# Four layers on 28x28 images: where first-layer moments, kernel sums and channel scales stand in rows 0 to 4, and when row 0's second turn is made

## The chip, the core and the metric

The kernel runs on one core of a Trainium2 chip. The metric is the device time of one execution in microseconds (us). The core's engines work side by side and meet at semaphores: TensorE (PE in the profile, with its weight loads as PEld), VectorE (DVE), ScalarE (ACT), GpSimd (POOL) and the DMA queue of SyncE (SP). Each engine takes its own instructions strictly in the order of the program, so a wait holds everything behind it on that engine.

## The reference

Eight images of 28x28 tokens and 64 channels go through four residual layers, each behind a group norm:

```python
x = x + _L0_conv_ref(_gn(x), ...)   # shifted-window attention, 7x7 windows, 8 heads
x = x + _L1_conv_ref(_gn(x), ...)   # 3x3 convolution of signs, scaled by K * alpha
x = x + _L2_conv_ref(_gn(x), ...)   # 3x3 convolution with ternary weights
x = x + _L3_conv_ref(_gn(x), ...)   # gated projection with a 4-tap convolution
```

The change lies in the first layer, with three small pieces that it computes:

- the moments (mean, variance) of the group norm ahead of layer 0;
- `alpha = jnp.mean(jnp.abs(kernel), axis=(0, 1, 2))` of layer 1, the mean absolute value of its kernel for each output channel, which needs the kernel only and not x;
- the attention itself: `softmax(q k + bias + mask) v`, then a projection.

## The kernel before

The images lie as four pairs (`g` = 0 to 3), a pair's two images on partitions 0 to 63 and 64 to 127. A pair has four window rows of four windows, so the first layer is a loop over 16 rows, `R` = 0 to 15, and each row has two turns, `k = 2R` and `2R + 1`, which stand for the two halves of the heads and use two buffers of scores in PSUM (`k % 2`).

For a row, the steps run over the engines in this manner:

- POOL: `normalise(R)` writes the normed input `xn`; `mask_row(R)` spreads the keys over heads into `kex` (line 214, called from the loop as `mask_row(R + 2)`).
- PE: `proj_qk(R)` (L791) and `proj_v(R)` (L803) project; `scores(R)` (L820) adds q k to both score buffers of the row; `turn(k, j)` (L833) transposes half j of the scores of turn k into the PSUM bank `turned j`; `values(k)` (L853) multiplies the exponentials with v into the bank `outs`; `gather(R)` (L867) and `project(R)` (L876) finish the row.
- ACT: `seed(k)` (L510) writes the bias into the score buffer of turn k, and may do so only once DVE has read the buffer for turn k - 2 (`sub_done`); `scores(R)` waits for both of its row's seeds. `expo(k, j)` (L540) takes the exponential of what `turn(k, j)` wrote. `evac_qk` (L519, L520), `evac_v` (L530) and `evac_att` (L549) empty PSUM.
- DVE: `shift(k)` subtracts the maximum (reduction `mx`, L1196, then `d`, L1201); `weigh(R)` (L1210, L1215) divides by the sums; `residual(R)` (L1226) adds to x.

The three pieces that move are all issued by DVE between these steps. `window_moments(g)` (L1123 twice, then L1130) takes the moments of pair g from the window copy `xw`; those of pairs 2 and 3 come after `weigh(0)` in row 1, and `gn_stats` is raised after the second. `variances(2, 2, 3, mixed)` in row 2 turns what PE's `mix` made of them into two variances (L1157, L1160, L1162), for a power on POOL. `kernel_sums()` (L1247) reduces the absolute kernel, which ACT wrote into `h1` in row 1, to `asum`. It comes right behind the variances in row 2. PE then makes `alpha` from `asum` with one matmul (L912, in row 3 behind `scores(4)`), in spare columns of the bank `turned 1`, which is why it waits until the exponential of the last turn there has been read (`exp_done`). `channel_scales()` (L1256 twice) copies `alpha` into `aw`; it is DVE's first step in row 4, and `turn(7, 1)` on PE, which overwrites that bank, waits for it (`aw_ready`). `aw` is used only behind the 16 rows, in `channel_sums`.

PE's order in a row R above 0 is: `turn(2R, 0)`, `turn(2R, 1)`, `values(2R - 1)`, `proj_v(R + 1)`, `scores(R + 1)`, `turn(2R + 1, 0)`, `turn(2R + 1, 1)`, `gather(R - 1)`, `values(2R)`, `proj_qk(R + 3)`, `project(R - 1)`. ACT's order in a row is: both `expo(2R, j)`, `evac_v(R + 1)`, both `expo(2R + 1, j)`, `evac_att(R - 1)`, `evac_qk(R + 3)`, `seed(2R + 4)`, `seed(2R + 5)`. In row 0 ACT has `seed(3)` and `evac_qk(2)` in the place of the first `evac_v`.

The order is written out by hand; no planner decides it.

Of the kernel before, what the change touches and what calls it, by code (L numbers as in the profile page):

```python
# [50 lines left out]
def program(nc, x_in, xw_in, cst_in, wts_in, late_in, ker1_in, ker2_in, rel_in, out):  # L51
    ctx = ExitStack()
    with ctx:
# [18 lines left out]
        def cc(name):  # L72
            a, n = CI[name]
            return cst[:, a:a + n]
# [44 lines left out]
        asum = sb("asum", [P, C])  # L119
# [30 lines left out]
        def sems(names):  # L150
# [12 lines left out]
        bqs_ready, pe_bt, bt_ready, kabs_ready, asum_ready, pe_alpha = sems(  # L163
            "bqs_ready pe_bt bt_ready kabs_ready asum_ready pe_alpha")
# [35 lines left out]
        NR = NG * NW  # L200
# [548 lines left out]
        def _(pe):  # L749
# [29 lines left out]
            def proj_qk(R):  # L779

                pe.wait_ge(xn_ready, R + 1)
                if R > 0:
                    pe.wait_ge(q_ready, R)
                    pe.wait_ge(ks_ready, R)
                if R > 0:
                    pe.wait_ge(v_ready, max(R - 1, 1))
                if R >= 4:
                    pe.wait_ge(att_ready, R - 3)
                rhs = xn[:, R % 4]
                for n, name in enumerate(("wq", "wk")):  # L790
                    mm = pe.matmul(ps_qk[:, n * RT:(n + 1) * RT], ww(name), rhs, start=True, stop=True)  # L791
                mm.then_inc(qk_done, 1)

            def proj_v(R):

                pe.wait_ge(xn_ready, R + 1)
                pe.wait_ge(q_ready, 1 if R == 0 else min(R + 2, NR))
                pe.wait_ge(ks_ready, 1 if R == 0 else min(R + 2, NR))
                if R == NR - 1:
                    pe.wait_ge(att_ready, R - 2)  # L800
                for a in range(NW):
                    for e in range(2):
                        mm = pe.matmul(ps_qk[64 * e:64 * e + WT, a * C:(a + 1) * C], xn[:, R % 4, a],  # L803
                                       ww("wv")[:, e * C:(e + 1) * C], start=True, stop=True)
                mm.then_inc(v_done, 1)
# [19 lines left out]
            def turn(k, j):  # L825
                pe.wait_ge(sub_done, k + 1)
                if k > 0:
                    pe.wait_ge(exp_done, 2 * k - 1 + j)
                if k == 7 and j == 1:
                    pe.wait_ge(aw_ready, 1)  # L830
                for n in range(4):
                    h = 8 * j + 2 * n
                    mm = pe.transpose(ps_t[j][0:WK, n * WQ:n * WQ + WK],  # L833
                                      d[0:WK, k % 2, h:h + 2, :].rearrange("p a b -> p (a b)")[:, 0:WK], packed)
                mm.then_inc(t_done, 1)

            def values(k):
                R, p = k // 2, k % 2
                pe.wait_ge(exp_done, 2 * k + 2)
                if p == 0:  # L840
                    pe.wait_ge(v_ready, R + 1)
                    if R > 0:
                        pe.wait_ge(o_ready, R)
                    if R > 1:
                        pe.wait_ge(res_done, R - 1)
                    pe.wait_ge(gn_copied, copied_by(R))

                for a in range(2):
                    for j in range(2):
                        for hp in range(2):  # L850
                            n = 8 * a + 4 * p + 2 * j + hp
                            for c in range(2):
                                mm = pe.matmul(ps_o[64 * c:64 * c + WT, 18 * n:18 * n + 18],  # L853
                                               pt[0:WK, k % 2, j, 2 * a + hp, WT * c:WT * c + WT],
                                               vsb[0:WK, R % 2, 2 * (4 * (2 * a + c) + 2 * j + hp) + p, :],
                                               start=True, stop=True)
                mm.then_inc(pv_done, 1)

            def gather(R):

                pe.wait_ge(o_ready, R + 1)
                pe.wait_ge(v_ready, min(R + 3, NR))
                if R >= NR - 2:
                    pe.wait_ge(att_ready, R)

                for m in range(NW // 2):
                    mm = pe.transpose(ps_qk[:, m * WQ:m * WQ + WK],  # L867
                                      osb[0:WK, 2 * m:2 * m + 2].rearrange("p a c -> p (a c)"), packed)
                mm.then_inc(ot_done, 1)

            def project(R):
                pe.wait_ge(att_ready, R + 1)
                pe.wait_ge(o_ready, R + 1)
                if R > 0:
                    pe.wait_ge(res_done, R)
                pe.matmul(ps_x, ww("wp"), att[:].rearrange("p i m j -> p (i m j)"), start=True, stop=True)\  # L876
                  .then_inc(proj_done, 1)
# [14 lines left out]
            for R in range(NR):  # L892
                g, r = R // NW, R % NW

                turn(2 * R, 0)
                turn(2 * R, 1)
                if R == 0:
                    proj_qk(2)
                if R == 2:
                    mix(2, 2, 3, mixed)  # L900
                if g > 0 and r == 2:
                    mix(col(1, g - 1), 1, nth(1, g - 1), mixed)
                if R > 0:
                    values(2 * R - 1)
                if 0 < R < NR - 1:
                    proj_v(R + 1)
                if R + 1 < NR:
                    scores(R + 1)
                if R == 3:
                    pe.wait_ge(asum_ready, 1)  # L910
                    pe.wait_ge(exp_done, 14)
                    pe.matmul(alpha, cc("ones"), asum[:], start=True, stop=True).then_inc(pe_alpha, 1)  # L912
                turn(2 * R + 1, 0)
                turn(2 * R + 1, 1)
                if R == 0:
                    proj_v(1)
                else:
                    gather(R - 1)
                values(2 * R)
                if R + 3 < NR:  # L920
                    proj_qk(R + 3)
                if R > 0:
                    project(R - 1)

            def conv_bank(u):

# [188 lines left out]
        def _(dve):  # L1115
# [4 lines left out]
            def window_moments(g):  # L1120

                for i in range(2):
                    last = dve.bn_stats(st[:, g % 2, i, :], xwflat[:, g, i * HALF:(i + 1) * HALF])  # L1123
                last.then_inc(bn_done, 1)
                dve.wait_ge(bn_done, g + 1)
                return merge(g % 2, col(0, g))
# [123 lines left out]
            def channel_scales():  # L1250

                dve.wait_ge(init_pool, 2)
                dve.wait_ge(pe_alpha, 1)
                for w in range(2):
                    q = slice(64 * w, 64 * w + 64)
                    last = dve.tensor_scalar(aw[q, 64 * w:64 * w + 64], alpha[q],  # L1256
                                             4.0 / (NTAP * C) / (NTAP * C), None, ALU.mult)
                last.then_inc(aw_ready, 1)
# [6 lines left out]
            for R in range(NR):  # L1265
                g, r = R // NW, R % NW

                if R == 4:
                    channel_scales()
                shift(2 * R)  # L1270
                shift(2 * R + 1)
                if R >= 1:
                    weigh(R - 1)
                if R >= 2:
                    if R == 2:
                        dve.wait_ge(ld_xu, 16)
                    residual(R - 2)
                if R == NR - 1 or g > 0 and r == 0:
                    dve.wait_ge(res_done, R - 1)
                    first_moments(g - 1 + (R == NR - 1))  # L1280
                if R == 0:
                    variances(1, 1, 2, mixed)
                if R == 1:
                    dve.wait_ge(ld_x2, 16)
                    window_moments(2)
                    window_moments(3).then_inc(gn_stats, 1)
                if R == 2:
                    variances(2, 2, 3, mixed)
                    kernel_sums()
                if g > 0 and r == 1:  # L1290

                    dve.wait_ge(res_done, R - 1)
                    last_moments(g - 1).then_inc(gn_stats, 1)
                if g > 0 and r == 2:
                    variances(col(1, g - 1), 1, nth(1, g - 1), mixed)
                if g > 0 and r == 3:
                    if g == 1:
                        dve.wait_ge(init_pool, 3)
                    signs(g - 1)
# [220 lines left out]
```

## Time and profile before

| | before |
|---|---|
| median of 3 runs | 196.95 us (196.94 to 197.01) |
| profiled execution, its own time | 196.93 us |
| span of its instructions | 195.1 us |
| PE busy | 182.3 us (93%) |
| DVE busy | 155.4 us (80%) |
| ACT busy | 128.3 us (66%) |
| POOL busy | 107.7 us (55%) |
| granted TensorE clock | 1.0 of full speed in every slice |

The 16 rows of the first layer take the span from about 15 to 119 us. The time of the profiled execution is 1.8 us more than the span, and that part lies outside all instructions. The shares are means over stages with different limits, so the stretch of rows 0 to 4 (15 to 50 us) has to be read by itself. In the rows of the timeline the columns are: start (us), busy time (us), engine, line, operation, output and inputs, count, and in brackets the idle time before it on that engine with what ended it. Where DVE instructions follow each other, the start of one may lie up to a tenth before the end of the one ahead.

### The profile page before, as it was taken

Reading aid. Unit: us, or ns where it says so; the run is one execution under the profiler, and the core shown is the slowest. Engines: PE = TensorE matmul, PEld = TensorE weight load, DVE = VectorE, ACT = ScalarE, POOL = GpSimd, SP = SyncE. Lnnn points to the kernel's source line nnn. Section 1 sums busy time; section 2 is a strip of 40 time slices with the busy share of each in tenths; the row PEclk is TensorE's granted clock in tenths of the full one; section 3 lists DMA queues with packets and bytes.
Section 4 is the critical chain, followed back from the end, with each engine's and each line's share of the span. In section 5 each row is a group of like instructions: output and inputs, shape, how many; then the busy total and the mean of one; then the engine's idle time right before and its main releaser. Section 6 shows DMA issues by size and latency. Waiting matters only on the chain.

```text
span 195.1 us, 6785 instructions
## 1 busy us (share of the span) xinstructions
PE 182.3 (93%) x2751; PEld 130.8 (67%) x2751; DVE 155.4 (80%) x322; ACT 128.3 (66%) x251; POOL 107.7 (55%) x122
## 2 busy tenths in 40 slices
PE   7876989989999999999999999998899999999994
PEld 2445878878898889889987886664456655453330
DVE  3568798978899788987898893799997768957653
ACT  3346778569767997777977757154965339789650
POOL 0339999958432479644595107749644410647560
PEclk9999999999999999999999999999999999999999
DMA  6990000000000000000000000002234521011512
GB/s 190 430 403 12 3 0 5 5 3 2 3 3 3 3 3 3 2 3 3 5 3 3 0 3 3 0 3 47 49 85 112 132 57 41 0 45 30 176 57 107
DMA packets 5021, 9.97 MB, mean 51 GB/s; under 512 B 768, under 2 KB 3840, under 8 KB 4864
## 3 DMA queue, kind: packets, MB, share of 16 engines
q1 hardware_dynamic: 4848, 9.21, 15.1%
q8 instruction: 22, 0.36, 0.7%
q10 hardware_dynamic: 144, 0.34, 0.4%
q14 instruction: 7, 0.06, 0.1%
HBM read 5.03 MB, written 1.61 MB: 34 GB/s over the span
## 4 chain that ended last, share of the span: by engine, by line
PE 74%; DVE 15%; issue 3%; POOL 3%; DMA 2%; ACT 2%; DVEq 0%; ACTq 0%; POOLq 0%
PE turned L833 13%; PE outs L853 12%; PE scores L954 7%; PE scores L820 6%; PE qkv L791 5%; PE turned L1036 4%; PE scores L1010 3%; PE scores L970 3%; PE qkv L803 3%; PE qkv L1024 3%; DVE mx L1196 3%; PE scores L1011 3%; DVE d L1201 3%; PE outs L876 2%; DMA xw<-xw_in 2%
## 5 line engine op out<-in xcount | busy, mean ns | idle before, releaser
L833 PE MATMUL turned<-cst,d 113*113 113x113 f32 x256 | 32.6, 270 | 2.3 <-DVE d L1201 2.0
L214 POOL TENSOR_TENSOR kex<-ks,cst 128x784 f32<-128x784 f32 (+1 forms) x16 | 23.6, 1472 | 19.9 <-ACT ks L519 19.3
L833 PEld LDWEIGHTS turned<-cst,d 113*113 113x113 f32 x256 | 28.6, 178 | 7.8 <-issue 4.7
L510 ACT ACTIVATE scores<-rel 113x784 f32<-113x784 f32 x32 | 26.0, 827 | 10.9 <-DVE d L1201 6.0
L540 ACT ACTIVATE pt<-turned 113x392 f32<-113x392 f32 x64 | 28.3, 493 | 6.3 <-PE turned L833 6.3
L1201 DVE TENSOR_TENSOR d<-scores,mx 113x784 f32<-113x784 f32 x32 | 31.2, 976 | 1.1
L1196 DVE TENSOR_REDUCE mx<-scores 113x16 f32<-113x784 f32 x32 | 30.7, 959 | 1.8 <-PE scores L820 1.7
L853 PE MATMUL outs<-vsb,pt 113*49 113x18 f32 x1024 | 29.2, 199 | 0.2 <-ACT pt L540 0.2
L853 PEld LDWEIGHTS outs<-vsb,pt 113*49 113x49 f32 x1024 | 26.1, 125 | 4.2 <-issue 0.6
L340 POOL TENSOR_TENSOR rstd<-ve,mhalf 128x1 f32<-128x1 f32 (+1 forms) x15 | 8.7, 580 | 24.3 <-DVE ve L1162 24.0
L249 POOL TENSOR_TENSOR kex<-su,sz 128x392 f32<-128x392 f32 x14 | 14.0, 1018 | 12.2 <-ACT su L664 7.1
L519 ACT ACTIVATE ks<-qkv,wts 128x196 f32<-128x196 f32 x16 | 6.8, 422 | 15.7 <-PE qkv L791 15.7
L820 PE MATMUL scores<-kex,qs 32*49 32x196 f32 x512 | 14.6, 332 | 2.4 <-ACT scores L510 1.9
L791 PE MATMUL qkv<-xn,wts 128*128 128x196 f32 x64 | 14.7, 352 | 0.3 <-ACT vsb L530 0.3
L1210 DVE RECIPROCAL rc<-outs 113x32 f32<-113x32 f32 x16 | 5.7, 358 | 10.9 <-PE outs L853 10.8
L939 PE MATMUL scores<-sg,w 128*128 128x392 bf16 x72 | 13.2, 332 | 0.5 <-DVE sg L1262 0.5
L1349 DVE SCALAR_TENSOR_TENSOR su<-scores,late,su 128x392 f32<-128x392 f32 x24 | 13.2, 619 | 0.4
L530 ACT ACTIVATE vsb<-qkv 49x256 f32<-49x256 f32 x32 | 12.6, 395 | 1.1 <-PE qkv L803 0.9
L377 POOL TENSOR_TENSOR h<-ab 128x840 f32<-128x840 f32 x4 | 6.3, 1586 | 12.6 <-ACT ab L558 12.5
L954 PE MATMUL scores<-p,w 128*64 128x392 bf16 x144 | 13.2, 334 | 0.0
L820 PEld LDWEIGHTS scores<-kex,qs 32*49 32x49 f32 x512 | 9.1, 117 | 4.7 <-issue 4.0
L1226 DVE SCALAR_TENSOR_TENSOR x<-outs,bt,x 128x175 f32<-128x175 f32 (+5 forms) x40 | 9.6, 290 | 1.9 <-PE outs L876 1.9
(130 smaller groups left out, 376.1 us busy)
## 6 DMA issues: line engine op xcount, KB each, us to landing
p<-parts SPq DMA_DIRECT2D x14, 112.5 KB, 2.2
x<-x_in SPq DMA_DIRECT2D x1, 1568.0 KB, 9.9
out<-xw SPq DMA_DIRECT2D x8, 196.0 KB, 1.9
xs<-xs SPq DMA_DIRECT2D x8, 98.5 KB, 2.1
xw<-xw_in SPq DMA_DIRECT2D x2, 392.0 KB, 4.7
xw<-xw_in SPq DMA_DIRECT2D x1, 784.0 KB, 6.6
ker<-ker_in SPq DMA_DIRECT2D x2, 288.0 KB, 10.3
p3x<-parts SPq DMA_DIRECT2D x8, 60.0 KB, 2.0
```

The lines of the kernel that those rows point to most:

```text
L214: return engine.tensor_tensor(kex[:, par, :, a * WT:b * WT], ks[:, a * WT:b * WT].rearrange("p (o t) -> p o t", o=1).broadcast_to([P, 4, n ...
L249: engine.tensor_tensor(yy[:, u % 4, :], su[:, u % 8], sz[:, u % 8], ALU.mult)\
L510: act.activation(o, i, ACT.Identity).then_inc(seeded, 1)
L540: act.activation(pt[0:WK, k % 2, j].rearrange("p n (w t) -> p n w t", w=2), ps_t[j][0:WK, 0:4 * WQ].rearrange("p (n w t) -> p n w t", n=4, ...
L791: mm = pe.matmul(ps_qk[:, n * RT:(n + 1) * RT], ww(name), rhs, start=True, stop=True)
L820: mm = pe.matmul(ps_s[w][64 * c:64 * c + WT, j, a * 4 * WT:(a + 1) * 4 * WT], qs[q, R % 2, m:m + WT], kex[q, R % 2, :, m:m + WT], start=Fa ...
L833: mm = pe.transpose(ps_t[j][0:WK, n * WQ:n * WQ + WK], d[0:WK, k % 2, h:h + 2, :].rearrange("p a b -> p (a b)")[:, 0:WK], packed)
L853: mm = pe.matmul(ps_o[64 * c:64 * c + WT, 18 * n:18 * n + 18], pt[0:WK, k % 2, j, 2 * a + hp, WT * c:WT * c + WT], vsb[0:WK, R % 2, 2 * (4 ...
L939: mm = pe.matmul(ps[:, 0:HALF], w1[:, tap, :], sg1[:, g, ky + i * HR:ky + (i + 1) * HR, kx:kx + HW], start=(tap == 0), stop=(tap == NTAP - 1))
L954: pe.matmul(ps[64 * w:64 * w + 64, 0:HALF], w2[:, tap], p12[:, g % 2, w, ky + i * HR:ky + (i + 1) * HR, kx:kx + HW], start=(tap == 0), sto ...
L1196: dve.tensor_reduce(top, sc, AXX, ALU.max).then_inc(max_done, 1)
L1201: dve.tensor_tensor(d[0:WK, s].rearrange("p (j m) t -> p j m t", j=2)[:, :, :, 0:WT], sc, top.rearrange("p j (m o) -> p j m o", o=1).broad ...
```

## The change

Five things move, and nothing is added or left out.

1. DVE takes `window_moments(2)` (with its wait for the load of pairs 2 and 3) in row 0 behind the variances of pair 1; `window_moments(3)` stays in row 1.
2. `kernel_sums()` goes from row 2 to the end of row 3.
3. `channel_scales()` goes from the front of row 4 to its end, behind `weigh(3)`, `residual(2)` and `first_moments(0)`. `turn(9, 1)` instead of `turn(7, 1)` waits for it.
4. PE's matmul for `alpha` goes from row 3, behind `scores(4)`, to row 4, ahead of `scores(5)`. It waits for `exp_done` 18, which is `expo(8, 1)`, where it waited for 14, `expo(6, 1)`.
5. In row 0 PE makes `turn(1, 0)` and `turn(1, 1)` ahead of `scores(1)`, not behind it.

```diff
@@ turn
-                if k == 7 and j == 1:
+                if k == 9 and j == 1:
                     pe.wait_ge(aw_ready, 1)
@@ the loop over rows, PE
                 if R == 0:
                     proj_qk(2)
+                    turn(1, 0)
+                    turn(1, 1)
+                    scores(1)
+                    proj_v(1)
+                    values(0)
+                    proj_qk(3)
+                    continue
...
-                if R > 0:
-                    values(2 * R - 1)
-                if 0 < R < NR - 1:
+                values(2 * R - 1)
+                if R < NR - 1:
                     proj_v(R + 1)
+                if R == 4:
+                    pe.wait_ge(asum_ready, 1)
+                    pe.wait_ge(exp_done, 4 * R + 2)
+                    pe.matmul(alpha, cc("ones"), asum[:], start=True, stop=True).then_inc(pe_alpha, 1)
                 if R + 1 < NR:
                     scores(R + 1)
-                if R == 3:
-                    pe.wait_ge(asum_ready, 1)
-                    pe.wait_ge(exp_done, 14)
-                    pe.matmul(alpha, cc("ones"), asum[:], start=True, stop=True).then_inc(pe_alpha, 1)
                 turn(2 * R + 1, 0)
                 turn(2 * R + 1, 1)
-                if R == 0:
-                    proj_v(1)
-                else:
-                    gather(R - 1)
+                gather(R - 1)
                 values(2 * R)
...
@@ the loop over rows, DVE
-                if R == 4:
-                    channel_scales()
                 shift(2 * R)
                 shift(2 * R + 1)
...
                 if R == 0:
                     variances(1, 1, 2, mixed)
-                if R == 1:
                     dve.wait_ge(ld_x2, 16)
                     window_moments(2)
+                if R == 1:
                     window_moments(3).then_inc(gn_stats, 1)
                 if R == 2:
                     variances(2, 2, 3, mixed)
+                if R == 3:
                     kernel_sums()
+                if R == 4:
+                    channel_scales()
```

## Rows read from the trace of the kernel before

**Rows 1.** Windows: stretch, its length, busy us of each engine (instructions), PEclk, DMA.
```profile
15.00:21.40 6.40, 4.91 (x100) 4.13 (x100) 5.43 (x9) 4.80 (x10) 6.04 (x9) 1.00 0.01 3
...
28.00:35.00 7.00, 6.52 (x136) 5.45 (x136) 6.41 (x14) 5.42 (x12) 6.72 (x5) 1.00 0.02 5
...
66.00:72.00 6.00, 6.00 (x137) 5.31 (x129) 5.32 (x10) 5.55 (x13) 2.68 (x2) 1.00 0.01 3
```
**Rows 2.** Timeline of row 0, ACT, DVE and PE.
```profile
17.05 0.83 ACT L510 ACTIVATE scores<-rel 113x784 f32<-113x784 f32 x1 [0.26 <-DVE d L1201]
...
17.19 0.98 DVE L1162 SCALAR_TENSOR_TENSOR ve<-sg 128x1 f32<-128x1 f32 x1
...
18.03 0.91 PE L820 MATMUL scores<-kex,qs 32*49 32x196 f32 x32 [1.12 <-ACT scores L510]
```
**Rows 3.** Timeline of row 1, PE and DVE.
```profile
21.93 0.98 DVE L1201 TENSOR_TENSOR d<-scores,mx 113x784 f32<-113x784 f32 x1
...
24.79 0.91 PE L820 MATMUL scores<-kex,qs 32*49 32x196 f32 x32 [0.27 <-ACT scores L510]
...
24.82 1.02 DVE L1123 BATCH_NORM_STATS2 st<-xw 128x6 f32<-128x392 f32 x2
...
27.15 0.92 DVE L1196 TENSOR_REDUCE mx<-scores 113x16 f32<-113x784 f32 x1
```
**Rows 4.** Timeline of row 2, PE, DVE and POOL.
```profile
29.13 1.05 PE L833 MATMUL turned<-cst,d 113*113 113x113 f32 x8 [0.23 <-DVE d L1201]
...
31.85 1.49 POOL L214 TENSOR_TENSOR kex<-ks,cst 128x784 f32<-128x784 f32 x1
...
32.80 0.57 DVE L1160 TENSOR_SCALAR negm<-sg 128x2 f32<-128x2 f32 x1
```
**Rows 5.** Chain that ended last, end of row 2: start us, us, what.
```profile
33.65 1.09 DVE asum L1247
```
**Rows 6.** Timeline of row 3 and of the front of row 4, PE, DVE and POOL.
```profile
38.67 0.73 POOL L340 TENSOR_TENSOR rstd<-ve,mhalf 128x2 f32<-128x2 f32 x1
...
39.35 0.54 DVE L1226 SCALAR_TENSOR_TENSOR x<-outs,bt,x 128x175 f32<-128x175 f32 x2
...
39.53 0.91 PE L820 MATMUL scores<-kex,qs 32*49 32x196 f32 x32 [0.48 <-ACT scores L510]
...
39.74 1.49 POOL L214 TENSOR_TENSOR kex<-ks,cst 128x784 f32<-128x784 f32 x1
...
40.37 0.43 PE L912 MATMUL turned<-asum,cst 128*128 128x64 f32 x2
...
40.64 0.60 PE L833 MATMUL turned<-cst,d 113*113 113x113 f32 x4
40.92 0.46 DVE L1256 TENSOR_SCALAR aw<-turned 64x64 f32<-64x64 f32 x2 [1.02 <-PE turned L912]
...
41.41 0.97 DVE L1196 TENSOR_REDUCE mx<-scores 113x16 f32<-113x784 f32 x1
...
41.52 0.62 PE L833 MATMUL turned<-cst,d 113*113 113x113 f32 x4 [0.28 <-DVE aw L1256]
```
**Rows 7.** Timeline of row 4 and of the front of row 5, PE, ACT and DVE.
```profile
44.21 0.96 PE L833 MATMUL turned<-cst,d 113*113 113x113 f32 x8
...
46.05 0.36 DVE L1210 RECIPROCAL rc<-outs 113x32 f32<-113x32 f32 x1 [0.78 <-PE outs L853]
...
46.20 0.88 ACT L540 ACTIVATE pt<-turned 113x392 f32<-113x392 f32 x2
...
46.42 0.91 PE L820 MATMUL scores<-kex,qs 32*49 32x196 f32 x32
...
47.27 1.05 PE L833 MATMUL turned<-cst,d 113*113 113x113 f32 x8
...
47.85 0.96 DVE L1196 TENSOR_REDUCE mx<-scores 113x16 f32<-113x784 f32 x1
...
50.38 0.95 PE L833 MATMUL turned<-cst,d 113*113 113x113 f32 x8
```

More of the change, by code:

```diff
@@ L921, in _ @@
                     proj_qk(R + 3)
-                if R > 0:
-                    project(R - 1)
+                project(R - 1)
             def conv_bank(u):
```

## The prediction

> **What bounds the kernel now.** I read the windows first. From 66 to 72 us PE is busy for 6.00 of 6.00 us: late in the 16 rows TensorE sets the pace, and an event that comes earlier there stays earlier to the end. From 28 to 35 us PE has idle time (6.52 of 7.00), while DVE holds 6.41 and POOL 6.72 [rows 1]. So time can be won in rows 0 to 4 alone, and only what is left of a gain when the PE-bound rows begin, at `turn(9)` and `turn(10)`, counts. The tempo to compare with is that of row 4: `turn(8)` 44.21, `scores(5)` 46.42, `turn(9)` 47.27, `turn(10)` 50.38 [rows 7], that is 2.21 + 0.85 + 3.11 = 6.17 us a row.
>
> The chain and the timeline then say what stands in the way in rows 0 to 4. In row 0 PE waits 1.12 us for `seed(3)` ahead of `scores(1)` [rows 2]. In row 1 DVE holds two window moments from 24.82 until `mx(4)` at 27.15, with `scores(2)` (24.79 + 0.91) long done [rows 3]; `turn(4)` on PE then waits for DVE [rows 4]. In row 2 `kernel_sums` alone takes 1.09 us of the chain [rows 5]. In row 3 PE loses 40.37 to 40.64 to the alpha matmul, and `turn(7, 1)` waits for `aw` until 41.52 [rows 6].
>
> **Row 0: the turn ahead of the scores.** `seed(3)` and `turn(1)` are released by the same `d(1)`; the seed runs from 17.05 to 17.88 and `scores(1)` starts at 18.03 [rows 2]. Put first, `turn(1)` fills PE from about 17.1 to 18.0, under the wait that is there anyway. So `scores(1)` stays at 18.0 to 18.05, and what stood behind it on PE (`proj_v(1)`, `values(0)`, `proj_qk(3)`, `turn(2)`) comes some 0.9 us earlier as far as its inputs allow. Its queue on ACT gains with it: `expo(1)` no longer waits for a late turn. Cost: nothing, with `seed(3)` as the cover; without that cover it would be 0.9 us of delay for `scores(1)`.
>
> **Row 0: the moments of pair 2.** Two window moments fill 24.82 to 27.15, so one costs 1.17 [rows 3]. Its wait for the load of pairs 2 and 3 costs nothing: from 15 us on the DMA engines are busy for 0.01 of the time [rows 1], so the load is in. Behind the variances, whose last instruction ends at 17.19 + 0.98 = 18.17, it ends at about 19.3. `scores(1)` is done at 18.03 + 0.91 = 18.94 [rows 2], so `mx(2)` comes 0.25 us later than now. That is all that it costs, and it goes down the DVE chain: `d(3)` ends at 22.91 + 0.25 = 23.15 [rows 3], `seed(5)` is 0.83 long as in [rows 2] and ends at 24.0, and `scores(2)` starts 0.15 later, at 24.15 instead of 24.79.
>
> **Row 1.** `mx(4)` now waits for `scores(2)` alone: 24.15 + 0.91 + 0.1 = 25.15, two us earlier than 27.15. With that `turn(4)` no longer waits for DVE; PE's own order sets it: 24.15 + 0.85 + 3.11 = 28.1 against 29.13 [rows 4, 7]. What is late next is PE, and the gain is 1.0.
>
> **Row 2: POOL's spread of the keys.** From `turn(4)` by way of `values(3)`, `weigh(1)` and `residual(0)` to `negm` of the variances are 3.67 us [rows 4]; moved, `negm` would start at 28.1 + 3.67 = 31.8. But now `negm` took 0.57 us for two columns, and it ended at 33.37, just behind POOL's `kex`, which ran from 31.85 to 33.34 [rows 4]. I read this as DVE being held until POOL was done, and POOL's instruction doesn't move: POOL is full there [rows 1] and nothing of its queue changes. The Trainium skill ("SBUF — State Buffer", its passage on reading the diagram of the two sides) says that DVE and GpSimd share a port pair as an exclusive lock, which a DVE instruction in a two-port mode or with two SBUF inputs needs; the 0.57 us bears this out, and by that rule the three variance instructions behind `sg` are held again. Without such a lock they would be over at about 32.4, and the time would be that of the first rival.
>
> So I take it that the variances end at about 33.65, as they do now [rows 5], whatever rows 0 to 2 have won before. What remains of the gain is that `kernel_sums` isn't there: `shift(6)` starts 1.09 us earlier. This is the main term. It also says that the reorder in row 0 and the moved moments win little by themselves: they buy room that ends at POOL. If `negm` slips in ahead of `kex` and only what follows it is held, another 0.1 is won.
>
> **Row 3.** `scores(4)` waits for `seed(9)`, that for `d(7)` [rows 6]; all of it moves by 1.09, to 38.44. `residual(1)` ends at 39.35 + 0.54 - 1.09 = 38.80 [rows 6], `kernel_sums` follows and ends at 39.89. `scores(4)` ends at 39.35, so `mx(8)` starts at 39.85 instead of 41.41, late by 0.4 against what it could be. The bounds of `kernel_sums` here are 0.7 (576 columns at the rate of `mx`, 0.97 us for 784 [rows 6]) and 1.17 us (as it ran, with the overlap of its neighbours); I take 1.09, the row itself. PE has lost its alpha matmul (0.27) and the wait of `turn(7, 1)`: half a turn from 40.64 ends at about 41.06, and it was held until 41.52, so 0.46. `turn(7)` is at 38.44 + 0.85 = 39.29 and `turn(8)` at 39.29 + 3.11 = 42.40, 1.8 us earlier than 44.21. What is late next is DVE and ACT.
>
> **Row 4: alpha in front of the scores.** This part takes most of it back. `mx(8)` at 39.85 and four instructions of 0.97 and 0.98 (with their overlap 3.88) give `d(9)` at 43.73; `seed(11)` ends at 44.60. Without alpha, `scores(5)` could start at 44.75. Now alpha stands in front and waits for `expo(8, 1)`, which ACT has only behind `seed(11)`: the pair of exponentials takes 0.88 [rows 7], so it ends at 45.4; with 0.1 for the semaphore alpha starts at 45.5, and 0.27 later [rows 6] `scores(5)` at 45.8. Queued behind on PE are `scores(5)` and both halves of `turn(9)`; on DVE `mx(10)` waits for it, at 46.8 (now 47.85 [rows 7]). The price is 1.05, bounded by 0.9 (the exponentials alone) and 1.2 (alpha at its full 0.43 [rows 6]). `turn(9)` starts at 45.8 + 0.85 = 46.65 against 47.27: the gain is 0.6 to 0.65.
>
> `turn(9, 1)`, half a turn later at 47.05, now waits for `aw`. `rc` of `weigh(3)` follows `turn(8)` by 1.84 and the end of `first_moments(0)` follows `rc` by 1.80 [rows 7]: 42.40 + 3.64 = 46.04. Alpha is there at 45.5 + 0.43 + 0.1 = 46.03, and `channel_scales` takes 0.46 [rows 6], though POOL's `kex` ran beside part of it: `aw` is ready for PE at 46.6, 0.4 us early. On DVE nothing is queued behind it but `shift(10)`, which waits for `scores(5)` anyway.
>
> **The sum.** Rows 0 to 2 bring 1.09 to `shift(6)`; in row 3 that grows to 1.56 at `mx(8)`, 1.8 at `turn(8)`; alpha gives back 1.05 to 1.15; at `turn(9)` 0.65 is left. From there on PE is busy throughout [rows 1], and all queues move together. The profiled execution took 196.93 us (span 195.1 and 1.8 around it; the median is 196.95): 196.93 - 0.65 = 196.3 us.
>
> **Rivals.**
>
> *The variances pass POOL.* If DVE reached `negm` some 0.5 us earlier than 31.8, or if the 0.57 us is no lock, variances end at about 32.4. Then row 3 is no longer tied to 33.65: `turn(6)` is PE's, at about 34.7, `mx(8)` at 38.9, and `turn(9)` 0.95 earlier than forecast. That gives 195.3. Against it is [rows 4], for it only that 31.8 and 31.85 are near each other.
>
> *`turn(9, 1)` waits for `aw`.* The wait of row 3 moves into row 4. It decides from 0.4 us of lateness on DVE. At the size of today (0.46 [rows 6]) the gain shrinks to 0.2: 196.7, no change. For it: four DVE steps stand in front, and alpha comes late; against it: the 0.4 us.
>
> *`kernel_sums` is held by POOL.* In row 3 it comes at 38.80, and POOL starts `rstd` at 38.67 and `kex` at 39.74 to 41.23 [rows 6]. Were the reduction, which reads SBUF, held like `negm` until that run is over, it would start 2.45 us late, and `mx(8)`, the seeds, alpha and `turn(9)` would follow one for one: 196.3 + 2.45 = 198.7, slower. It decides from whether a reduction with one SBUF input needs what POOL holds, and from its coming behind 38.67. Against it: 1.09 us beside a POOL that is busy for 6.72 of 7.00 us [rows 1, 5]. The Trainium skill ("VectorE: DVE Perf Modes", the perf-mode tier table) has a reduction in the one-port mode only, which speaks against it too.
>
> **How the numbers follow.** Forecast 0.64, variances pass 0.10, `aw` wait 0.18, `kernel_sums` held 0.08. The forecast's own range is 196.0 (0.1 from `negm`, 0.15 from alpha at its lower bound) to 196.6 (alpha at 1.2 and `mx(2)` felt later on). The range goes from 195.8 to 196.9, which takes in the forecast and the `aw` wait and leaves out most of the other two. A measurement of this kernel can tell 0.2% (0.4 us) from no change. Faster by more: 0.70, from the forecast without its upper edge (0.60) and the first rival; within: 0.22, from the `aw` wait and that edge; slower: 0.08.
>
> **What would show it.** `scores(1)` at 18.0 behind `turn(1)`; `mx(2)` at 19.3; `turn(4)` near 28.1; `negm` or `ve` ending at POOL's 33.34; `mx(6)` at 33.6; a PE wait of about 0.9 us ahead of L912 at 45.5, ended by ACT's exponential; no wait at `turn(9, 1)`; `turn(9)` near 46.6. It is wrong if `mx(6)` starts before 33, if alpha doesn't wait, or if rows 5 to 15 lose the gain again.

## The result and the profile after

The changed kernel took 195.57 us (four executions, 195.43 to 195.60) against 196.94 for the kernel before: a ratio of 0.9929, with an interval of 0.9911 to 0.9946. That is 1.37 us faster. 196.3 had been forecast, in a range of 195.8 to 196.9, and the time of the first rival was 195.3: the direction was right, the range missed the time by 0.23 us on the fast side, and the case that came was the one given a chance of 0.10. The profiled execution took 195.60 us with a span of 193.8.

A later set of twelve executions of the same kernel (changed_again, below) gave 196.06 against 196.97, a ratio of 0.9951 (0.9943 to 0.9960). The 196.06 lies inside the forecast's range, and only one of the times, 195.45, is like those of the first set. What sorts these times is the main question of this text. The sets of runs were taken on several chips, on which the kernel before took 196.94 to 197.06, so differences of about 0.1 us between sets say nothing. In the sets below, executions in which the granted clock fell under 0.995 (one here, three of ten in port_free, two of ten in sums_in_row2) are left out of the groups that are named, since they are 1 to 2.5 us longer.

The windows of the kernel after, with the same columns as [rows 1]:

```profile
28.00:35.00 7.00, 7.00 (x145) 6.43 (x144) 5.58 (x13) 5.68 (x13) 6.72 (x5) 1.00 0.02 5
35.00:41.50 6.50, 6.50 (x141) 5.75 (x140) 5.80 (x10) 4.53 (x11) 6.18 (x6) 1.00 0.02 5
41.50:48.00 6.50, 5.04 (x130) 4.26 (x129) 5.34 (x11) 4.79 (x11) 4.59 (x9) 1.00 0.02 4
```

PE is now busy from 28 to 41.5 us without a gap (6.52 of 7.00 in the first stretch before), and then idles for 1.5 us: that is row 4.

The timeline of rows 0 and 1 after, answering to [rows 2, 3, 4]. `seed(3)` starts at 17.27 here and at 17.05 before, so 0.22 us of each time below is only a later start of everything:

```profile
17.29 1.05 PE L833 MATMUL turned<-cst,d 113*113 113x113 f32 x8 [0.16 <-DVE d L1203]
...
18.27 0.91 PE L820 MATMUL scores<-kex,qs 32*49 32x196 f32 x32
...
19.50 0.92 DVE L1198 TENSOR_REDUCE mx<-scores 113x16 f32<-113x784 f32 x1
...
24.33 0.91 PE L820 MATMUL scores<-kex,qs 32*49 32x196 f32 x32 [0.47 <-ACT scores L510]
...
25.34 0.96 DVE L1198 TENSOR_REDUCE mx<-scores 113x16 f32<-113x784 f32 x1
...
28.28 0.96 PE L833 MATMUL turned<-cst,d 113*113 113x113 f32 x8
```

The turn stands in front of `scores(1)`, which starts at once behind it; `mx(4)` is 2.0 us earlier than before, `turn(4)` 1.1, both counted from `seed(3)`.

Row 2 after, answering to [rows 4]:

```profile
31.86 0.20 DVE L1162 TENSOR_SCALAR negm<-sg 128x2 f32<-128x2 f32 x1
31.93 0.34 DVE L1164 SCALAR_TENSOR_TENSOR ve<-sg 128x1 f32<-128x1 f32 x2
32.11 1.53 POOL L214 TENSOR_TENSOR kex<-ks,cst 128x784 f32<-128x784 f32 x1
32.19 0.97 DVE L1198 TENSOR_REDUCE mx<-scores 113x16 f32<-113x784 f32 x1
...
34.81 0.96 PE L833 MATMUL turned<-cst,d 113*113 113x113 f32 x8
```

Here the forecast parts from what happened. `negm` takes 0.20 instead of 0.57, both `ve` are over at 32.27, and it is POOL's spread of the keys that is a little longer (1.53 against 1.49). `mx(6)` starts at 32.19 and not at 33.82, which is the forecast's 33.6 with the later start. The prediction had named `mx(6)` before 33 as a sign that it was wrong.

Rows 3 and 4 after, answering to [rows 6, 7]:

```profile
37.85 1.16 DVE L1249 TENSOR_REDUCE asum<-h 128x64 f32<-128x576 f32 x1
...
38.92 0.96 DVE L1198 TENSOR_REDUCE mx<-scores 113x16 f32<-113x784 f32 x1
...
40.04 1.50 POOL L214 TENSOR_TENSOR kex<-ks,cst 128x784 f32<-128x784 f32 x1
...
41.63 0.42 ACT L519 ACTIVATE ks<-qkv,wts 128x196 f32<-128x196 f32 x1 [1.91 <-POOL kex L214]
...
42.26 1.57 ACT L510 ACTIVATE scores<-rel 113x784 f32<-113x784 f32 x2
...
43.75 0.88 ACT L540 ACTIVATE pt<-turned 113x392 f32<-113x392 f32 x2
...
44.77 0.41 PE L916 MATMUL turned<-asum,cst 128*128 128x64 f32 x2 [1.46 <-ACT pt L540]
...
45.11 0.91 PE L820 MATMUL scores<-kex,qs 32*49 32x196 f32 x32
45.29 0.46 DVE L1258 TENSOR_SCALAR aw<-turned 64x64 f32<-64x64 f32 x2 [0.53 <-PE turned L916]
...
45.96 1.05 PE L833 MATMUL turned<-cst,d 113*113 113x113 f32 x8
```

Alpha waits 1.46 us for the exponential, with `scores(5)` queued behind it, while the seeds were done at 43.83. `turn(9)` goes through in one piece, since `aw` is ready at 45.75. It comes 1.53 us earlier than before (45.96 against 47.27, and the 0.22 of the start).

### The profile page after: what moved, and what is told of

It reads as the page before. It is cut to its first block, busy times and chain, and to the rows that moved or that the text cites. A ratio compares the mean times of both kernels' runs of the same rounds, so it can differ in the third digit from the quotient of the medians.

```text
span 193.8 us, 6785 instructions
## 1 busy us (share of the span) xinstructions
PE 182.7 (94%) x2751; PEld 131.0 (68%) x2751; DVE 154.9 (80%) x322; ACT 128.0 (66%) x251; POOL 107.8 (56%) x122
## 4 chain that ended last, share of the span: by engine, by line
PE 80%; DVE 12%; POOL 3%; issue 2%; ACT 2%; ACTq 0%; DVEq 0%; POOLq 0%
PE turned L833 14%; PE outs L853 13%; PE scores L820 7%; PE scores L956 7%; PE qkv L791 6%; PE turned L1038 4%; PE scores L1012 3%; PE scores L972 3%; PE qkv L803 3%; PE qkv L1026 3%; PE outs L876 3%; PE scores L765 3%; PE scores L1013 3%; DVE mx L1198 2%; DVE d L1203 2%
## 5 line engine op out<-in xcount | busy, mean ns | idle before, releaser
L803 PE MATMUL qkv<-wts,xn 128*49 128x64 f32 x256 | 10.2, 221 | 1.0 <-ACT qs L520 1.0
```

## Experiments

Two theories stood against each other. One: POOL holds DVE's variances if it comes first, and the whole surplus over the forecast is that in this kernel DVE came first by a tenth of a us. The other: nothing is held, and the gain is simply PE's and DVE's earlier work.

**late_variances** puts DVE half a us later at the point of meeting.

```diff
                 if R == 2:
+                    dve.bn_stats(st[:, 1, 1, :], xwflat[:, 2, 0:HALF])
                     variances(2, 2, 3, mixed)
```

> The changed kernel with one more statistics instruction of 0.51 us on DVE ahead of the variances of pairs 2 and 3 in row 2; its result goes to a buffer that nobody reads any more. In the changed kernel the three variance instructions run from 31.86 to 32.27 and POOL's spread of the keys starts at 32.11. Theory (DVE only passed POOL by a tenth, and is held by it if it comes second): negm starts near 32.4, one of the variance instructions ends at POOL's end (33.65), mx(6) starts near 33.9 instead of 32.19, turn(6) near 36.0 instead of 34.81, turn(9) near 46.9 instead of 45.96, and the time is 196.4 to 196.6. Rival (nothing holds DVE; the 0.57 us of before was something else): mx(6) starts 0.5 later at 32.7, d(6) ends at 34.7, just in time for turn(6) at 34.81, and the time stays at 195.6 to 195.7.

Measured: 196.37 us (196.27 to 196.58), ratio 0.9967 (0.9955 to 0.9978). Its timeline in row 2:

```profile
31.52 0.56 DVE L1288 BATCH_NORM_STATS2 st<-xw 128x6 f32<-128x392 f32 x1
...
31.93 1.49 POOL L214 TENSOR_TENSOR kex<-ks,cst 128x784 f32<-128x784 f32 x1
32.00 0.15 DVE L1159 TENSOR_TENSOR sg<-outs,epsv 128x6 f32<-128x6 f32 x1
32.18 1.27 DVE L1162 TENSOR_SCALAR negm<-sg 128x2 f32<-128x2 f32 x1
...
33.36 0.37 DVE L1164 SCALAR_TENSOR_TENSOR ve<-sg 128x1 f32<-128x1 f32 x2
...
33.65 0.96 DVE L1198 TENSOR_REDUCE mx<-scores 113x16 f32<-113x784 f32 x1
...
35.68 1.05 PE L833 MATMUL turned<-cst,d 113*113 113x113 f32 x8 [0.86 <-DVE d L1203]
```

`negm`, 0.17 to 0.20 us long when free, takes 1.27 and ends at 33.45, behind POOL's 33.42. Counted from `seed(3)` (17.12 here), half a us of delay became 1.6 at `mx(6)`; `turn(6)` then waits 0.86 us for DVE, and 0.8 is left in the time, against the first set of the changed kernel. `sg`, which reads PSUM, ran beside the same POOL instruction in 0.15 us without being held; the statistics did too, but had started ahead of it. The rival (195.6 to 195.7) is out.

**row0_as_before** undoes the reorder alone: `scores(1)` again ahead of `turn(1)`.

```diff
                     proj_qk(2)
-                    turn(1, 0)
-                    turn(1, 1)
                     scores(1)
+                    turn(1, 0)
+                    turn(1, 1)
                     proj_v(1)
```

> The changed kernel with row 0 in the old order: scores(1) ahead of turn(1). Theory (the reorder is what brings DVE past POOL): turn(4) comes near 29.0 instead of 28.28, negm near 32.5, behind the start of POOL's spread at 32.1, is held until 33.65, and the time is 196.3 to 196.6, so that the reorder by itself is worth 0.8 to 1.0 us. Rival, as in the prediction (the reorder only buys room that is lost later): 195.6. Third case (the reorder is worth its PE time, without any holding): turn(6) 0.6 later and 196.0 to 196.2.

Measured: 196.40 us (196.26 to 196.49), ratio 0.9966 (0.9954 to 0.9978). `negm` starts at 32.43, POOL at 31.99, and `negm` is held for 1.07 us. Against the first set of the changed kernel the reorder is worth 0.8, and 0.3 against the later one (196.06), where a part of the variances is held as well. So the prediction's "win little by themselves" is wrong for it where DVE passes. The trace shows the hold; what the old order would cost without one was not run.

**moments_in_row1** undoes the move of `window_moments(2)` alone.

```diff
                 if R == 0:
                     variances(1, 1, 2, mixed)
+                if R == 1:
                     dve.wait_ge(ld_x2, 16)
                     window_moments(2)
-                if R == 1:
                     window_moments(3).then_inc(gn_stats, 1)
```

> The changed kernel with window_moments(2) back in row 1, beside that of pair 3; row 0 keeps its new order. mx(4) then waits for DVE until about 26.5 instead of 25.34 and turn(4) comes 0.2 to 0.3 later, which puts negm at about 32.1, level with POOL's spread. Theory (this part is worth what it does for that meeting): DVE comes second in most executions and the time is 196.2 to 196.5, with 195.6 to 195.8 where it comes first. Rival (the part is worth nothing, PE covers it): 195.4 to 195.6.

Measured: 196.28 us (196.10 to 196.40), ratio 0.9963 (0.9951 to 0.9976). `negm` starts at 31.90 and POOL at 31.93; `negm` takes 0.17 us and the two `ve` take 1.59. Against changed_again, of the same set of runs, that is 0.22 us, with a hold in both. The 0.7 against the first set is therefore mostly the difference between the changed kernel's own two times, and it isn't shown that this move decides between them.

**sums_in_row2** undoes the move of `kernel_sums`, the prediction's main term.

```diff
                 if R == 2:
                     variances(2, 2, 3, mixed)
-                if R == 3:
                     kernel_sums()
```

> The changed kernel with kernel_sums back in row 2, right behind the variances; alpha and the channel scales stay in row 4. The prediction called this move the main term, 1.09 us: by that the time would be 196.6. Theory now: in row 2 it delays mx(6) by 1.09, but turn(6) only by 0.5, since PE is the later one there; in row 3 it is gone and mx(8) waits for scores(4) instead of it; seeds, alpha and turn(9) come 0.3 to 0.4 later than in the changed kernel, and the time is 195.9 to 196.0.

Measured: a median of 197.18 us, ratio 0.9996 (0.9968 to 1.0024), but in two groups: three executions at 195.74 to 195.92 and five at 197.0 to 197.27. The profiled one is of the second group (197.2):

```profile
31.75 0.17 DVE L1162 TENSOR_SCALAR negm<-sg 128x2 f32<-128x2 f32 x1
31.82 1.66 DVE L1164 SCALAR_TENSOR_TENSOR ve<-sg 128x1 f32<-128x1 f32 x2
31.97 1.49 POOL L214 TENSOR_TENSOR kex<-ks,cst 128x784 f32<-128x784 f32 x1
...
33.40 1.14 DVE L1249 TENSOR_REDUCE asum<-h 128x64 f32<-128x576 f32 x1
```

`negm` got through, and the second of the two `ve` was held until POOL's 33.46 (they end at 33.48). The same program is faster or slower by 1.3 us, with POOL starting 0.22 us behind `negm` here and 0.25 in the kernel after. The lower group fits the 195.9 expected for a free DVE; that it was free there is inferred from the time, since no trace of that group was taken.

**changed_again** is the changed kernel without an edit.

> The changed kernel, unaltered, in more executions. In four executions DVE's variances passed POOL's spread of the keys by a tenth of a us and the time was 195.4 to 195.6; in sums_in_row2 the same meeting went both ways in one kernel (195.8 or 197.1). Theory (a meeting so near goes both ways by chance): most executions at 195.4 to 195.6, and those that lose it near 196.4, as late_variances. Rival (in this kernel DVE always wins): all at 195.4 to 195.6.

Measured: 196.06 us, ratio 0.9951 (0.9943 to 0.9960). One execution took 195.45, nine 195.90 to 196.15, one 196.37. The profiled one took 195.92:

```profile
31.57 0.17 DVE L1162 TENSOR_SCALAR negm<-sg 128x2 f32<-128x2 f32 x1
31.65 1.63 DVE L1164 SCALAR_TENSOR_TENSOR ve<-sg 128x1 f32<-128x1 f32 x2
31.78 1.49 POOL L214 TENSOR_TENSOR kex<-ks,cst 128x784 f32<-128x784 f32 x1
33.21 0.96 DVE L1198 TENSOR_REDUCE mx<-scores 113x16 f32<-113x784 f32 x1
...
35.23 1.05 PE L833 MATMUL turned<-cst,d 113*113 113x113 f32 x8 [0.55 <-DVE d L1203]
```

POOL follows `negm` by 0.21 us, and a `ve` is held. The meeting does go both ways, as the first theory has it, but the expectation failed: most executions took neither of its two times. The middle case (`negm` passes and only what is behind it is held) stands in the prediction, at 0.1 us, and I left it out of the expectation. Counted from `seed(3)`, `mx(6)` starts 0.3 us earlier here than in late_variances. By these times the change brings 1.4 us where all three pass, and 0.9 where a `ve` is held; only two of the fifteen executions have a trace. All four of the first set took 195.43 to 195.60, and one of eleven of the second did, so it is not an even chance from one execution to the next; what differed between the sets is not known.

**port_free** takes away what holds DVE: POOL's sign weights leave rows 1 and 2, and its spread of the keys runs three us earlier.

```diff
...
-                if R == 1:
-                    binary_signs()
-                if R == 2:
+                if R == 3:
                     ternary_signs()
                 if R == 4:
+                    ternary_rest()
                     tap_weights()
+                if R == 5:
+                    binary_signs(0)
+                if R == 9:
+                    pool.wait_ge(xn_ready, R + 5)
+                    binary_signs(1)
```

> The changed kernel with POOL's sign weights moved out of rows 1 and 2 (the binary halves to rows 5 and 9, the ternary steps to rows 3 and 4). POOL's spread of the keys for row 4 then runs near 28.6 to 30.1, long before DVE's variances at 31.9, so that nothing is left there to meet. Theory: every execution has the variances free; ACT's emptying of the keys of row 6 no longer waits for POOL (it did for 1.91 us of idle time, of which 0.7 beyond PE), but scores and alpha in row 4 are then bound by d(9), so only 0.1 to 0.2 is won: 195.35 to 195.55. Rival (POOL's full queue is a bound of its own in rows 2 to 4): below 195.2.

Measured: a median of 195.46 us, ratio 0.9941 (0.9915 to 0.9967); the seven executions at a clock of 0.998 or more took 195.19 to 195.53, one group. So ACT's wait for POOL ahead of row 6's keys, 1.91 us of idle time in the profile after, is worth no more than 0.2.

**late_variances_port_free** is that and late_variances together.

> As port_free, with the additional 0.51 us statistics instruction of late_variances ahead of the variances. Theory (late_variances lost 0.8 us because POOL held DVE, not because DVE was later): with POOL's spread gone from that place the delay costs nothing, since PE is the later one at turn(6): 195.35 to 195.7. Rival (the half us of DVE itself is what cost): 196.2 to 196.4, as late_variances.

Measured: 195.47 us (195.33 to 195.65), ratio 0.9917 (0.9902 to 0.9932). Its row 2:

```profile
32.45 0.17 DVE L1169 TENSOR_SCALAR negm<-sg 128x2 f32<-128x2 f32 x1
32.53 0.34 DVE L1171 SCALAR_TENSOR_TENSOR ve<-sg 128x1 f32<-128x1 f32 x2
32.79 0.97 DVE L1205 TENSOR_REDUCE mx<-scores 113x16 f32<-113x784 f32 x1
...
34.93 0.95 PE L840 MATMUL turned<-cst,d 113*113 113x113 f32 x8
```

The same half us of DVE costs 0.8 with POOL's `kex` in the way and nothing without (195.47 against 195.46). So what made it dear is POOL's instruction in that place, and not DVE's lateness.

**alpha_behind_scores** prices the other disputed term by putting alpha behind `scores(5)`.

```diff
-                if R == 4:
-                    pe.wait_ge(asum_ready, 1)
-                    ...
                 if R + 1 < NR:
                     scores(R + 1)
+                if R == 4:
+                    pe.wait_ge(asum_ready, 1)
+                    ...
```

> The changed kernel with alpha behind scores(5) instead of ahead of it; turn(9, 1) still waits for the channel scales. Theory (alpha ahead of the scores costs PE a wait of over one us for the exponential): scores(5) starts near 44.0 instead of 45.11, alpha near 44.8, turn(9) near 45.1, its second half waits for the channel scales until about 45.9 where it started at 46.4, and the time is 195.0 to 195.2. Rival (the wait only stands where another one would: the scores or the channel scales are late anyway): 195.5 to 195.7.

Measured: 195.12, 195.15, 195.65 and 195.76 us, ratio 0.9918 (0.9901 to 0.9935). The two upper times fit a held `ve`, which was not traced. In the profiled execution (195.12) the variances pass POOL, and row 4 goes:

```profile
43.90 0.91 PE L820 MATMUL scores<-kex,qs 32*49 32x196 f32 x32 [0.64 <-ACT scores L510]
...
44.74 0.43 PE L918 MATMUL turned<-asum,cst 128*128 128x64 f32 x2
45.01 0.60 PE L833 MATMUL turned<-cst,d 113*113 113x113 f32 x4
...
45.89 0.62 PE L833 MATMUL turned<-cst,d 113*113 113x113 f32 x4 [0.28 <-DVE aw L1258]
```

`scores(5)` is 1.2 us earlier; a turn that waits for `aw`, as in [rows 6], takes more than half of that back: the lower two times are 0.45 us under the changed kernel's first set.

**alpha_at_the_end** moves alpha into row 15, behind `turn(30)`, into a bank of scores that is free by then, and `channel_scales` behind `shift(31)`.

```diff
-        alpha = ps_t[1][:, 4 * WQ:4 * WQ + C]
+        alpha = bk[0][:, 0:C]
...
+                if R == NR - 1:
+                    pe.wait_ge(asum_ready, 1)
+                    pe.matmul(alpha, cc("ones"), asum[:], start=True, stop=True).then_inc(pe_alpha, 1)
...
                 shift(2 * R + 1)
+                if R == NR - 1:
+                    channel_scales()
```

> The changed kernel with the alpha matmul in row 15 between turn(30) and values(29), where PE waits for DVE anyway, in a free bank, and the channel scales behind shift(31); no turn waits for them any more. Theory (alpha ahead of scores(5) costs a wait for the exponential): scores(5) starts near 44.0 instead of 45.11, turn(9) near 44.85 instead of 45.96, rows 5 to 15 keep that, and the time is 194.4 to 194.7. Rival (another wait takes its place in row 4 or in rows 14 and 15): 195.2 to 195.6.

Measured: 195.13 us (194.96 to 195.21), ratio 0.9898 (0.9883 to 0.9913). It missed its expectation (194.4 to 194.7). In the profiled execution a `ve` was held (1.64 us); without that hold, and with POOL's keys early as well, alpha_end_port_free came to 194.24. Against the held group of changed_again (196.06) alpha is worth 0.93.

**alpha_end_port_free** is that with port_free.

> alpha_at_the_end with POOL's sign weights out of the way as in port_free, so that the variances are never held. Theory: port_free had scores(5) at 44.97 because of alpha; without alpha seed(11) sets it, near 43.85, and the time is 195.4 less 1.1: 194.2 to 194.5. Rival (the wait in row 4 only changes its name): 194.9 to 195.2, as alpha_at_the_end.

Measured: 194.24 us (194.21 to 194.47), ratio 0.9863 (0.9851 to 0.9876), 1.1 to 1.2 us under port_free. `scores(5)` starts at 43.71, behind `seed(11)`.

**all_three** adds `kernel_sums` in row 4.

```diff
-                if R == 3:
+                if R == 4:
                     kernel_sums()
```

> alpha_at_the_end and port_free together, with kernel_sums in row 4 instead of row 3. Theory: from turn(4) on PE is busy throughout, 6.17 us a row, so that turn(10) comes near 47.3 instead of 49.07, and the time is 193.8 to 194.2. Rival (ACT or DVE in row 3 or 4 is the next to be late): 194.4 to 194.7, as alpha_at_the_end.

Measured: 194.56 us (194.49 to 194.70), ratio 0.9871 (0.9857 to 0.9886). The rival's time came, by DVE: it is slower than alpha_end_port_free, since in row 4 the reduction stands in front of `mx(10)`, and `turn(10)` waits for `d(10)` by 0.41 us (47.44).

**sums_under_cover** puts `kernel_sums` where DVE waits, ahead of `weigh(1)` in row 2, and ACT's absolute values ahead of `evac_qk(4)`.

```diff
+                if R == 2:
+                    kernel_sums()
                 if R >= 1:
                     weigh(R - 1)
...
```

> alpha_end_port_free with kernel_sums in row 2 ahead of weigh(1), where DVE waits 1.28 us for values(3), and ACT's absolute values of the kernel one step earlier in row 1, ahead of evac_qk(4), where ACT waits for PE. Theory: nothing but PE is left in rows 2 to 5 (turn(8) near 40.9, turn(9) near 43.9, turn(10) near 47.0), and the time is 193.4 to 193.8. Rival (DVE's or ACT's moved step comes late and pushes the row): 194.2 to 194.6.

Measured: 193.85 us (193.68 to 193.93), ratio 0.9838 (0.9824 to 0.9852), the fastest of all, and 0.05 us above what was expected. The timeline of its rows 2 and 4:

```profile
28.59 1.49 POOL L214 TENSOR_TENSOR kex<-ks,cst 128x784 f32<-128x784 f32 x1 [0.97 <-ACT ks L526]
29.06 1.17 DVE L1253 TENSOR_REDUCE asum<-h 128x64 f32<-128x576 f32 x1
30.42 0.36 DVE L1216 RECIPROCAL rc<-outs 113x32 f32<-113x32 f32 x1 [0.19 <-PE outs L858]
...
40.96 0.96 PE L838 MATMUL turned<-cst,d 113*113 113x113 f32 x8
...
43.18 0.91 PE L827 MATMUL scores<-kex,qs 32*49 32x196 f32 x32
...
44.02 1.05 PE L838 MATMUL turned<-cst,d 113*113 113x113 f32 x8
...
47.13 0.96 PE L838 MATMUL turned<-cst,d 113*113 113x113 f32 x8
```

The reduction fills DVE's wait, and its neighbour `kex` on POOL does not hold it. From `turn(8)` to `turn(10)` PE runs at the pace of [rows 7], 6.17 us (40.96 to 47.13), with nothing in front of it.

## Why the prediction was wrong, step by step

*Rows 0 and 1.* Right to 0.05 us. With 0.22 added for the later start, `scores(1)` was foreseen at 18.27 (18.27), `mx(2)` at 19.52 (19.50), `scores(2)` at 24.37 (24.33), `mx(4)` at 25.37 (25.34), `turn(4)` at 28.32 (28.28).

*Row 2, the step that failed.* The step that failed is "the three variance instructions behind `sg` are held again", and with it the variances' end at 33.65, "whatever rows 0 to 2 have won before". In the profiled execution none of the three was held, and they ended at 32.27. The mechanism, that one engine holds the other, was right, and its outcome was called wrongly. `negm` was put at 31.8 and POOL at 31.85, so that by the prediction's own numbers DVE came first. Two things were off. `turn(4)` to `negm` took 3.58 us and not 3.67: the row of before had started that turn out of a wait for DVE, and it lasted 1.05 there and 0.96 without one. With the 0.04 by which `turn(4)` was early and rounding, `negm` came 0.16 earlier than written.

And the first rival was said to need 0.5 us more, as if all three had to be over when POOL starts. It needs only that each instruction of DVE starts before POOL's does, and `negm` and both `ve` start within some 0.2 us. The Trainium skill ("SBUF — State Buffer", on reading the diagram) has just that: the one that starts first gets the pair for its whole instruction. The prediction used that rule without asking who comes first. The traces agree for a DVE that comes second (1.27 us for `negm` in late_variances). For a POOL that comes second they don't show a wait: `kex` took 1.53 and 1.54 instead of 1.49 where the last `ve` overlapped it by 0.16 to 0.18 us (the kernel after, alpha_behind_scores), and 1.49 beside the rest of `negm` in moments_in_row1. Two times 0.05 us apart, from rows good to 0.1, should have been given like chances, and not 0.64 against 0.10.

*The middle case was sized too small.* "If `negm` slips in ahead of `kex` and only what follows it is held, another 0.1 is won": in changed_again that came, and `mx(6)` was 0.3 us earlier than with a held `negm`. Most of the later executions have the time of this case, so their 196.06 lies inside the range by a term that was three times too small; that agreement is luck.

*The forecast's case was worked out correctly.* Where POOL holds `negm`, the kernels took 196.37 (late_variances) and 196.40 (row0_as_before), and 196.3 was forecast. These are kernels with one edit; their variances end with POOL, as the forecast had it. Counted from `seed(3)`, late_variances has `scores(4)` at 38.45 (38.44 was forecast), `turn(8)` at 42.41 (42.40), `scores(5)` at 45.81 (45.8) and `turn(9)` at 46.65 (46.65). The first rival's case was, too: with the 0.22 it had `turn(6)` at 34.9 (34.81), `turn(9)` at 45.9 (45.96), and 195.5 us (195.60 for the profiled execution).

*The main term.* `kernel_sums` was sized at 1.09 us, by holding the rest fixed at POOL. By the lower group of sums_in_row2 its move is worth 0.3 where DVE is free; that PE is then the later one at `turn(6)` is argued, since that group has no trace. In the upper group it is worth about 1.1 against changed_again's 196.06, so the size was right for a held DVE.

*Row 4, alpha.* Right in kind and size: 1.05 was foreseen, 1.1 to 1.2 (alpha_end_port_free against port_free) and 0.93 (alpha_at_the_end against changed_again) were measured. The wait that PE sees is longer in the kernel after (1.46 instead of 0.9), since it comes to it earlier; where the variances were held it is 0.79 to 0.81 (late_variances, changed_again).

*The `aw` rival* did not come: `turn(9)` had no wait. Where alpha stands behind the scores it does (0.28 in alpha_behind_scores).

*The `kernel_sums` rival* is out: the reduction took 1.16 and 1.17 us beside POOL in the kernel after and in sums_under_cover.

*What was missed.* ACT's wait for POOL's spread of row 5's keys, ahead of emptying row 6's (1.91 us idle), was not foreseen. port_free shows it to cost 0.2 at most, as `d(9)` comes nearly as late.

## What to carry to other kernels

Where two engines meet within a tenth of a us at something that only one of them can hold, the time of the kernel is a choice between two or more values, and all should be in the range with like chances; here moving POOL's work away made it one value again. A matmul that needs a bank freed by a later stage should not stand in front of the work that the next row waits for: it is cheapest where its engine waits in any case. The same holds for a reduction: under a wait it left PE's pace as it was, and two rows later the kernel took 0.6 to 0.7 us more (all_three against sums_under_cover, which also moves ACT's absolute values).

## What the runs showed of the hardware that was not expected

One kernel can have times that lie 0.3 to 1.3 us apart at one granted clock (changed_again, sums_in_row2): with POOL starting 0.24 or 0.25 us behind `negm` both `ve` passed (alpha_behind_scores, the kernel after), with 0.20 to 0.22 one was held (alpha_at_the_end, changed_again, sums_in_row2). The offset moves on POOL's side. From `seed(3)` to `negm` DVE took 14.58 or 14.59 us in all five traces, whose programs are alike up to there; POOL's fills of row 1, from their first to the next `kex`, took 4.15 and 4.16 us in the two that passed and 4.12 to 4.14 in the three that were held. Why these fills differ by 0.04 us between executions stays open.

Instructions of one and two columns, 0.17 to 0.21 us long when free, took much longer behind a single instruction of a neighbour engine: `negm` with two columns 1.07 to 1.27 us, two `ve` together 1.59 to 1.66 instead of 0.34. The kernel before shows it in row 0 as well, which the prediction did not use: the `ve` of [rows 2], 0.98 us long, ends at 18.17 with POOL's 18.15, while `negm` with one column goes through beside the same POOL instructions.

```profile
16.30 1.85 POOL L332 TENSOR_TENSOR rel<-rel,cst 128x392 f32<-128x392 f32 x2
...
17.12 0.15 DVE L1160 TENSOR_SCALAR negm<-sg 128x1 f32<-128x1 f32 x1
```

So not every small instruction is held. Nor was `sg`, which reads PSUM (0.15 us in late_variances), and the reduction `asum` took 1.14 to 1.17 us in every run, whichever POOL instruction ran beside it.
